# Decoder of two layers on one core: the first mixture's routing moved into the MLP, its rows merged back by VectorE

## Chip, core, metric
One core of one Trainium2 chip. The metric is the device time of one execution in microseconds, from the program's start to its end. Lower is better. The program is one hand-written instruction stream per engine (TensorE, VectorE, ScalarE, GpSimd, SyncE), with semaphores between them.

## What is computed
x is [4, 512, 256] (2048 tokens of 256), the context [4, 1601, 256], all fp32. Two layers, each of a Mamba mixer, a cross attention and a feed-forward, with residuals and norms between them. The change is around the first layer's feed-forward, a mixture of eight experts with one expert for each token and room for 512 tokens in each:

```python
x_flat = (x_normed @ W_proj + b_proj).reshape(N, d)
routing_weights = softmax(x_flat @ W_gate)
ew, ei = top_k(routing_weights, 1); ew = ew / ew.sum()        # weight of the one choice
masked = where(ei == e, ew, -1); top_scores, top_idx = top_k(masked, 512)   # per expert
h = gelu(layernorm(x_flat[top_idx] @ W1 + b1)); out_e = h @ W2 + b2
outputs = zeros.at[top_idx].add(out_e * w)
x = x + layernorm(outputs) * ln_g + ln_b
```

Ahead of it stands the first layer's cross attention with its own MLP (256 to 1024 to 256 with a gelu), behind it the second layer's Mamba mixer: projection, convolution with 4 taps, silu, x projection, dt (softplus), a scan over 512 tokens for 512 channels x 16 states, gate, output projection.

## The kernel before
**Order.** `build` (L3415) strings seven stages, with a barrier between two: mixer A (0 to 555 us), keys of the first attention (to 970), queries and MLP (to 1278), experts of the first mixture (to 1609), mixer B (to 2145), second attention (to 2540), second mixture. `barrier` (L3409) drains each engine and waits for all five, so what is issued behind a barrier, a DMA too, starts only then. SBUF tiles and semaphores of a stage are given on to the next.

**MLP and gate** (`queries_pe`, `queries_dve`, `queries_act`, L1212 to L1501). Per batch of 512 tokens TensorE makes 8 hidden products, then 4 output tiles; woven in are the gate's steps of the batch before: transposes of the normalized rows (`gate_turned_pe`, at hidden product 4), projection to XF, transposes of XF, logits. VectorE begins a batch with the statistics of X (`x_stats_dve`), the affine rows of the next batch (`rows2`), the reciprocal, and the gate's normalized rows fn. Behind the loop stands the last batch's gate, with nothing beside it.

**Routing** (`experts_dve` L2039 to L2073, `ranks_pe`). After the barrier, for all 16 tiles of 128 tokens at once: first maximum, one-hot marks, softmax weight (Exp on ScalarE), ranks by two products with a triangle and with ones, running totals by 15 dependent adds, slot number, two lists of indices. GpSimd scatters 16 tiles of XF into m0buf by indirect DMA (L1805), SP waits for all (L1787) and loads expert 0's rows. Before this SP has issued both weights of expert 0.

**Expert loop** (`experts_pe`, `experts_act`, `experts_dve`). Every product is three fp32r products of high and low halves (`mm3`, L107). Per expert: W1 and W2 are cast to high halves by ScalarE and the low halves made by VectorE; 4 hidden tiles of [128, 1024] are drawn by VectorE with b1 (L2017) and their statistics taken (L2022); `hidden_norm` normalizes them (L2037); 8 times transposes, gelu and cast on ScalarE (L1945, L1950), low half on VectorE (L2098); 4 output tiles, drawn with b2 to ob (L2114), stored by ScalarE's queue to m0res in slot order. The hidden products of the next expert are woven between the transposes of this one.

**Merge** (L1808 to L1814, L2117 to L2150). GpSimd waits for all stores, then gathers 16 tiles of XF from m0res by indirect DMA. ScalarE multiplies by the weight, VectorE takes statistics, normalizes with ln_g, adds to X, and takes the statistics of the new X for mixer B.

**Mixer B's start** (`mamba_sp`, `mamba_dve`, `mamba_act`, `mamba_pe`). After the barrier SP loads the four weights; TensorE waits for the last of them (L393). Normalized rows xn, transposes, input projection of four blocks, four convolutions on VectorE (`mamba_conv_dve`, 4 operations each), silu, x projection, dt, softplus, first decays, then the scan of 128 units with VectorE at 3.46 us each. B and C rows go to DRAM and come back broadcast over partitions, by SP.

## Time and profile before

| what | us |
|---|---|
| median of 3 runs (lowest, highest) | 2915.48 (2909.48, 2918.29) |
| the profiled execution's own time | 2914.07 |
| its span, first to last instruction | 2912.2 |
| TensorE busy | 2417.0 (83%) |
| VectorE busy | 2194.8 (75%) |
| ScalarE busy | 1444.4 (50%) |
| GpSimd busy | 894.5 (31%) |
| granted TensorE clock, mean | 0.910 of full |
| chain that ended last | PE 49%, DVE 28%, ACT 10%, issue 8%, POOL 2%, DMA 1% |

The sum of a forecast is made against 2914.07. PE is TensorE, DVE VectorE, ACT ScalarE, POOL GpSimd, SP SyncE; a name with q is the engine's queue. "L1805" is a line of the kernel before. out<-in are tile names without their numbers. A busy share says little where stages have different bounds: the chain and the windows by stage say more.

### The profile page before, as it was taken

The numbers are of one execution on the slowest core, as the hardware profiler recorded it, in microseconds if no ns is written. First come the engines' busy times: TensorE is split into PE (matmuls) and PEld (weight loads), VectorE is DVE, ScalarE is ACT, GpSimd is POOL, SyncE is SP. The second block draws the span as 40 slices with busy tenths as digits, with TensorE's granted clock in tenths as the row PEclk, the third lists the DMA queues.
The fourth block names the chain that finished last, engine by engine and source line by source line (L and its number), as shares of the span: only waits on it lengthen the run. The fifth ranks groups of instructions, "written<-read, shape, count | busy, mean of one in ns | idle before, by whom it ended". The sixth has DMA issues, their size and how long they took to land.

```text
span 2912.2 us, 31513 instructions
## 1 busy us (share of the span) xinstructions
PE 2417.0 (83%) x10888; PEld 1575.3 (54%) x10888; DVE 2194.8 (75%) x3180; ACT 1444.4 (50%) x2547; POOL 894.5 (31%) x617
## 2 busy tenths in 40 slices
PE   4989886588998899947993698988668888899998
PEld 1333332266776565736993233343234443799998
DVE  4999999688997365336995599999956653567776
ACT  5666564254665222213673565656412445356663
POOL 2868776300000000020002377877611235100004
PEclk7999999899999799978997699999987887889999
DMA  4031130380000000023331303203054231246652
GB/s 171 1 116 55 62 117 0 118 288 23 23 1 1 35 1 1 0 89 112 110 129 44 139 4 112 98 19 117 0 81 94 51 100 59 86 149 218 218 207 91
DMA packets 99065, 243.12 MB, mean 83 GB/s; under 512 B 9182, under 2 KB 63339, under 8 KB 91740
## 3 DMA queue, kind: packets, MB, share of 16 engines
q1 hardware_dynamic: 82540, 216.20, 22.7%
q10 hardware_dynamic: 11760, 12.32, 1.6%
q0 software_dynamic: 4608, 12.59, 1.4%
q8 instruction: 87, 1.43, 0.2%
q14 instruction: 70, 0.57, 0.1%
HBM read 187.93 MB, written 46.66 MB: 81 GB/s over the span
## 4 chain that ended last, share of the span: by engine, by line
PE 49%; DVE 28%; ACT 10%; issue 8%; POOL 2%; DMA 1%; ACTq 0%; DVEq 0%; SPq 0%; POOLq 0%
DVE psum L635 11%; PE psum L109 6%; PE psum L111 6%; PE psum L432 6%; PE psum L110 6%; PE psum L116 3%; DVE ch L643 3%; PE psum L397 3%; ACT WH L3119 2%; PE psum L1265 2%; PE psum L1279 2%; ACT g L3266 2%; PE psum L1249 2%; PE psum L2575 1%; PE psum L1227 1%
## 5 line engine op out<-in xcount | busy, mean ns | idle before, releaser
L317 POOL TENSOR_TENSOR bu<-u,row 128x1024 f32<-128x1024 f32 x254 | 597.0, 2355 | 289.0 <-DVE psum L635 190.9
L432 PE MATMUL psum<-ch,ident 128*128 128x512 f32 x1024 | 510.1, 627 | 137.9 <-DVE ch L643 137.3
L635 DVE TENSOR_TENSOR_SCAN psum<-psum,bu 128x1024 f32<-128x1024 f32 x256 | 585.5, 2287 | 18.8 <-ACT psum L514 18.6
L432 PEld LDWEIGHTS psum<-ch,ident 128*128 128x128 f32 x1024 | 188.5, 196 | 426.7 <-DVE ch L643 245.0
L514 ACT ACTIVATE psum<-dt,A 128x511 f32<-128x511 f32 x512 | 332.4, 682 | 0.4
L643 DVE TENSOR_TENSOR ch<-psum,row 128x1024 f32<-128x1024 f32 x256 | 313.0, 1223 | 7.6
L1535 POOL IOTA i<- 128x128 f32 x1 | 0.3, 345 | 710.2 <-DVEq L3411 710.2
L397 PE MATMUL psum<-hT,inw 128*128 128x512 f32 x256 | 140.7, 682 | 42.8 <-ACT sz L474 27.3
L3266 ACT ACTIVATE g<-psum,bias 128x256 f32<-128x256 f32 x248 | 101.2, 470 | 133.7 <-PE psum L111 126.0
L109 PE MATMUL psum<-WH,hs 128*128 128x256 f32 x496 | 145.3, 293 | 4.7 <-DVE hs L3346 2.3
L109 PE MATMUL psum<-xT,WH 128*128 128x256 f32 x496 | 142.3, 287 | 7.6 <-DVE xT L3309 7.6
L111 PE MATMUL psum<-xT,WH 128*128 128x256 f32 x496 | 141.7, 286 | 0.0
L110 PE MATMUL psum<-xT,WH 128*128 128x256 f32 x496 | 141.6, 286 | 0.0
L3346 DVE TENSOR_TENSOR hs<-g,hs 128x512 fp32r<-128x512 f32 x124 | 85.6, 693 | 73.5 <-ACT hs L3273 71.4
L111 PE MATMUL psum<-WH,hs 128*128 128x256 f32 x496 | 140.8, 284 | 0.0
L110 PE MATMUL psum<-WH,hs 128*128 128x256 f32 x496 | 140.3, 283 | 0.0
L3088 POOL DMA_INDIRECT R<-m1res,gi x26 | 26.2, 1007 | 340.0 <-DMA m1res<-ob 323.8
L511 ACT COPY psum<-zero 128x2 f32<-128x2 f32 x256 | 41.2, 161 | 175.3 <-DVE ch L643 174.4
L2650 ACT ACTIVATE pT<-psum 128x1024 f32<-128x1024 f32 (+3 forms) x128 | 87.5, 706 | 76.6 <-PE psum L2560 76.0
L2863 POOL TENSOR_SCALAR_AFFINE_SELECT pT<-pT 128x256 f32<-128x256 f32 x128 | 53.5, 422 | 230.6 <-ACT pT L2650 229.5
L3127 DVE TENSOR_TENSOR WH<-W,WH 128x1024 fp32r<-128x1024 f32 x96 | 113.1, 1220 | 7.8 <-ACT WH L3119 7.8
L397 PEld LDWEIGHTS psum<-hT,inw 128*128 128x128 f32 x256 | 54.2, 217 | 116.5 <-issue 63.7
(403 smaller groups left out, 5907.6 us busy)
## 6 DMA issues: line engine op xcount, KB each, us to landing
W<-in_m1W SPq DMA_DIRECT2D x24, 2052.0 KB, 8.6
row<-Ascr SPq DMA_DIRECT2D x64, 512.0 KB, 4.8
row<-Bscr SPq DMA_DIRECT2D x64, 512.0 KB, 4.8
m1buf<-zt SPq DMA_DIRECT2D x8, 2048.0 KB, 16.7
W<-in_m0W SPq DMA_DIRECT2D x16, 1024.0 KB, 5.0
xe<-m1buf SPq DMA_DIRECT2D x23, 256.0 KB, 8.2
m1res<-ob ACTq DMA_DIRECT2D x23, 256.0 KB, 5.0
m0buf<-zt SPq DMA_DIRECT2D x16, 256.0 KB
```

What stands on the lines that cost most here:

```text
L109: pe.matmul(o, al, bh, start=start, stop=False)
L110: pe.matmul(o, ah, bl, start=False, stop=False)
L111: return pe.matmul(o, ah, bh, start=False, stop=stop)
L317: e.tensor_tensor(m.bu[i % 3][:, :, :], u, m.row[:, g, 0, :, :], ALU.mult).then_inc(*m.fed.up)
L397: p = pe.matmul(bank, m.inw[:, f, 128 * ob:128 * ob + 128], m.hT[:, f, :], start=f == 0, stop=f == 1)
L432: p = pe.matmul(m.y, k.ident, m.ch[i % RING_C][:, j, :], start=False, stop=g == UNITS - 1 and j == 1)
L514: e = act.activation(a[:, j, 1:T], m.dt[:, s % SIX, 1:T], ACT.Exp, scale=m.A[:, n:n + 1])
L635: dve.tensor_tensor_scan(flat, flat, m.bu[i % 3][:, :, :].rearrange("p a n -> p (a n)"), 0.0, ALU.mult, ALU.add).then_inc(*m.scan.up)
L643: dve.tensor_tensor(m.ch[i % RING_C][:, :, :], a, m.row[:, g, 1, :, :], ALU.mult).then_inc(*m.out.up)
L2650: act.activation(m.pT[n % 6][:, :, 0:W], m.st[n % 2][:, :, 0:W], ACT.Exp, scale=0.25).then_inc(*m.ex.up)
L3127: dve.tensor_tensor(lo, w, hi, ALU.subtract).then_inc(*m.Wl.up)
L3266: e = act.activation(g[:, 256 * o:256 * o + 256], m.hb[j][:, 256 * o:256 * o + 256], ACT.Gelu_apprx_tanh, bias=m.bias[w % 3][:, 2 * j + o: ...
```

## The change
1. **Choice per batch in the MLP.** `gate_marks_dve`, `gate_exp_act`, `gate_ranks_pe`, `gate_slots_dve` do the routing of batch b-1 inside the MLP's iteration b (marks after logits, slots after the last output tile, ranks behind TensorE's last output tile) and of the last batch behind the loop, ahead of the barrier. GpSimd scatters batches 0 to 2 in the MLP (`mlp_pool`), batch 3 after the barrier.
2. **XF and m0buf rows get two columns**, the token's weight and its home number, and travel with the row.
3. **Expert 0's W1 and W2** are loaded in the MLP, when the last attended tile is out.
4. **The final norm moves to the experts' rows.** The weighted row's norm is taken on ob (statistics on VectorE, scale w/dev with the variance taken as w*w*var, applied by ScalarE; for the last expert by VectorE), and GpSimd scatters each expert's four tiles straight to their tokens' rows in m0res, which was cleared to zero. Half of the hidden normalization goes from VectorE to ScalarE. X + ln_b is added during expert 7.
5. **Mixer B** loads m0res as four blocks, VectorE multiplies with ln_g and adds to X; batch 0 first, batches 1 to 3 after the convolutions. Its weights are loaded during expert 2.
6. **Both mixers** make the fourth convolution on TensorE.
7. **First loads before the barrier**: wk, the first three context tiles and two ln rows for the keys, wk and the first context of the second attention.

```diff
@@ queries_dve, end of an MLP iteration
         out(4 * b + 2, bank["t2"])
         if b:
             gate_logits_dve(k, g, dve, b - 1, bank["lg"])
+            gate_marks_dve(k, g, dve, b - 1)
         out(4 * b + 3, bank["t3"])
+        if b:
+            gate_slots_dve(k, g, dve, b - 1, bank["rk"])
...
+def mlp_pool(k, m, g, pool):
+    gate_consts_pool(k, g, pool)
+    for b in range(B - 1):
+        gate_scatter_pool(k, g, pool, b)
...
+def gate_marks_dve(k, m, dve, b):
...
+    first_of_four_dve(k, m, dve, m.lg[:, s, :], m.m1[:, s], m.oh[:, s, :])
+    dve.tensor_scalar(m.end[:, :], m.ix[:, :], float(CAP), float(CAP * (E + 1)), ALU.mult, ALU.add).then_inc(*m.marks.up)
+    dve.tensor_tensor(m.sm[:, :, :], m.lg[:, s, :], wide4(m.m1[:, s]), ALU.subtract).then_inc(*m.sm_in.up)
...
+def gate_slots_dve(k, m, dve, b, bank):
+    dve.wait_ge(*m.sm_exp(b))
...
+    dve.wait_ge(*m.counted(b))
+    for t in range(4):
+        n = 4 * b + t
+        dve.tensor_tensor(m.tot[:, n + 1, :], m.tot[:, n, :], bank[:, 32 + E * t:32 + E * t + E], ALU.add).then_inc(*v.up)
+        done()
...
+    dve.tensor_tensor(m.XF[:, s, D], m.ws[:, :], m.keep[:, s], ALU.mult)
+    dve.tensor_copy(m.put_i[:, s], m.slot[:, s]).then_inc(*m.put.up)
@@ experts_pool
+    def tags(e):
+        pool.wait_ge(*m.xe_in(e))
...
+        pool.tensor_tensor(m.tf[:, e, :], m.room[:, e, :], m.xe[:, :, D + 1], ALU.add).then_inc(*m.tf_in.up)
+        pool.tensor_copy(m.tw[:, e, :], m.xe[:, :, D])
+        pool.tensor_tensor(m.t2[:, e, :], m.xe[:, :, D], m.xe[:, :, D], ALU.mult)
+        pool.tensor_scalar(m.tn[:, e, :], m.xe[:, :, D], -1.0, None, ALU.mult)
+        pool.wait_ge(*m.tf_in(e))
+        pool.tensor_copy(m.ti[:, e, :], m.tf[:, e, :]).then_inc(*m.tagged.up)
...
+    for e in range(E):
+        if e + 2 < E:
+            tags(e + 2)
+        if e:
+            out_scale(e - 1)
+            pool.wait_ge(*m.o_n(e - 1))
+            for t in range(4):
+                out_home(e - 1, t)
+        if e + 1 < E:
+            out_var(e)
+    for t in range(4):
+        pool.wait_ge(*m.o_last(t))
+        out_home(E - 1, t)
@@ hidden_norm on ScalarE and VectorE
+        for t in (2, 3):
+            h = m.hN[e % 2][:, t, :]
+            a = act.activation(h, h, ACT.Identity, scale=m.hrs[e % 2][:, t:t + 1], bias=m.hnb[e % 2][:, t:t + 1])
...
+        for t in range(2):
+            normed(dve, hN[:, t, :], hN[:, t, :], mv, m.hrs[e % 2], t).then_inc(*m.h_n.up)
@@ experts_sp
+        if e == 2:
+            mamba_weights_sp(k, following, sp)
+    for home in m.home:
+        sp.wait_ge(*home(2 * E - 1))
@@ mixer B
+def mamba_home_dve(k, m, dve, b):
+    x, rows = k.X[:, 4 * b:4 * b + 4, :], mamba_home(m, b)
+    dve.wait_ge(*m.home_in[b](0))
+    dve.tensor_tensor(rows, rows, k.zt[:, 0:1, :].to_broadcast([128, 4, D]), ALU.mult).then_inc(*m.times.up)
+    dve.wait_ge(*m.times(b))
+    dve.tensor_tensor(x, x, rows, ALU.add).then_inc(*m.home.up)
+    dve.wait_ge(*m.home(b))
+    x_stats_dve(k, dve, 4 * m.rnd + b)
...
-    for ob in range(4):
+    for ob in range(3):
         mamba_conv_dve(k, m, dve, ob)
+    if m.rnd:
+        for j in range(1, B):
+            mamba_home_dve(k, m, dve, j)
@@ mamba_act, unit loop
+        if m.rnd and i == 1:
+            for j in range(1, B):
+                x_stats_act(k, act, 4 * m.rnd + j)
```

`mamba_home` is the region of the B/C rows, in which the four blocks of m0res land before those rows are loaded; SP waits for the last addition before it goes on.

## Rows read from the trace of the kernel before
**Rows 1.** Windows of MLP, expert loop, second hole: stretch, length, PE PEld DVE ACT POOL busy, PEclk, DMA.
```profile
1125.00:1268.00 143.00, 137.87 (x562) 97.04 (x562) 54.69 (x144) 39.56 (x55) 0.00 (x0) 0.98 0.00 1
...
1340.00:1561.00 221.00, 210.50 (x1407) 192.20 (x1405) 183.01 (x290) 139.19 (x189) 0.00 (x0) 0.97 0.32 111
1561.00:1602.00 41.00, 0.00 (x0) 0.00 (x0) 29.10 (x97) 9.77 (x23) 16.71 (x16) 0.52 0.22 64
```

**Rows 2.** The chain of waits, routing. Columns: start us, us, what.
```profile
1278.13 0.19 DVE lg L1751
...
1281.09 1.28 ACT L1929
...
1284.12 0.17 DVE tot L1574
...
1310.27 2.40 DMA m0buf<-XF,puti
1312.68 3.70 DMA xe<-m0buf
```

**Rows 3.** The chain of waits, merge and second mixer's start.
```profile
1559.79 1.43 DVE ob L2114 x4
...
1616.26 3.80 PE psum L397 x4
```

**Rows 4.** Timeline of GpSimd, its third scatter. Columns: start us, us, engine, line, operation, idle.
```profile
1292.84 1.95 POOL L1805 DMA_INDIRECT m0buf<-XF,puti  x1 [0.30 <-issue]
```

**Rows 5.** The chain of waits, first loads of both attentions.
```profile
555.87 4.90 DMA gT<-in_x0wk
...
2145.10 3.86 DMA cT<-in_x1ctxT
```

**Rows 6.** Timeline of VectorE beside GpSimd: keys' start, routing.
```profile
565.51 2.15 DVE L904 SCALAR_TENSOR_TENSOR XF<-XF,cmv,bc 128x256 f32<-128x256 f32 x1
...
1289.28 2.41 DVE L1992 TENSOR_TENSOR W1s<-W,W1s 128x1024 fp32r<-128x1024 f32 x2
```

**Rows 7.** Timeline of VectorE in the MLP, third and fourth batch.
```profile
1197.88 1.38 DVE L150 TENSOR_SCALAR fn<-X,xmv,xrs 128x256 f32<-128x256 f32 x4
...
1233.08 0.18 DVE L140 RECIPROCAL xrs<-xsd 128x4 f32<-128x4 f32 x1 [3.62 <-ACT xsd L146]
```

**Rows 8.** Timeline of TensorE in the MLP and behind its end.
```profile
1200.29 1.04 PE L116 MATMUL psum<-ident,fn 128*128 128x128 f32 x8
...
1241.73 3.62 PE L1683 MATMUL psum<-wp,fT 128*128 128x256 f32 x16
...
1265.13 1.55 PE L116 MATMUL psum<-ident,fn 128*128 128x128 f32 x8 [3.31 <-DVE fn L150]
1267.52 6.34 PE L1683 MATMUL psum<-wp,fT 128*128 128x256 f32 x16 [0.83 <-ACT fT L1707]
```

**Rows 9.** Timeline of VectorE across one expert boundary.
```profile
1423.17 2.98 DVE L150 TENSOR_SCALAR hN<-hN,hmv,hrs 128x1024 f32<-128x1024 f32 x4
...
1435.32 0.69 DVE L2098 TENSOR_TENSOR hs<-g,hs 128x512 fp32r<-128x512 f32 x1 [0.57 <-ACT hs L1950]
```

**Rows 10.** Timeline of all engines at the program's start.
```profile
0.82 2.10 SPq L3475 DMA_DIRECT2D X<-in_x  x4
...
4.97 1.41 DVE L129 BATCH_NORM_STATS2 xst<-X 128x6 f32<-128x256 f32 x4 [4.97 <-DMA X<-in_x]
```

**Rows 11.** Groups by line in the expert loop, ScalarE's cast of 128x1024.
```profile
L1908 ACT CAST W1s<-W 128x1024 fp32r<-128x1024 f32 x12 | 11.9, 1039 | 0.0
```

**Rows 12.** Timeline of VectorE, second mixer's start.
```profile
1609.70 1.39 DVE L150 TENSOR_SCALAR xn<-X,xmv,xrs 128x256 f32<-128x256 f32 x4 [0.33 <-DVEq L3411]
...
1629.74 2.33 DVE L330 SCALAR_TENSOR_TENSOR xc<-xs,PV,xc 128x512 f32<-128x512 f32 x3
1646.13 0.69 DVE L297 TENSOR_TENSOR dt<-dt,xs 128x512 f32<-128x512 f32 x1 [14.06 <-ACT xs L482]
...
1652.39 2.30 DVE L635 TENSOR_TENSOR_SCAN psum<-psum,bu 128x1024 f32<-128x1024 f32 x1 [3.19 <-ACT psum L514]
```

More of the change, by code:

```diff
@@ L205, in mamba_make @@
     n = PER * B
-    m.w = c(L + "weights", 4, 16)
+    m.w = k.next_w if rnd else c(L + "weights", 4, 16)
+    if rnd:
+        m.home_in, m.home = [c(L + f"rows_home{b}", 1, 16) for b in range(B)], c(L + "x_plus_rows", B)
+        m.times = c(L + "rows_times", B)
     m.zeros = c(L + "zeroed", 2)
@@ L281, in mamba_sp, with mamba_home @@
     sp.dma_start(m.outw[:, :, :], d[L + "outw"]).then_inc(*m.w.up)
+def mamba_home(m, b):
+    return m.row[:, b, 0, :, :].rearrange("p a (t c) -> p (a t) c", c=D)
+def mamba_sp(k, m, sp):
+    if m.rnd:
+        for b in range(B):
+            sp.dma_start(mamba_home(m, b), k.DR["m0res"][T * b:T * b + T, :].rearrange("(t p) c -> p t c", p=128)).then_inc(*m.home_in[b].up)
+        sp.wait_ge(*m.home(B - 1))
+    else:
+        mamba_weights_sp(k, m, sp)
     for b in range(B):
@@ L637, in mamba_dve @@
             mamba_gate_dve(k, m, dve, s - 1)
+        if m.rnd and i == 4:
+            for j in range(1, B):
+                x_inverse_dve(k, dve, 4 * m.rnd + j)
         if n == 5 and b + 1 < B:
+            if m.rnd:
+                dve.wait_ge(*k.inv_dev(4 * m.rnd + b + 1))
             mamba_rows_dve(k, m, dve, b + 1)
@@ L1630, in ffn0_make @@
[L1630 to L1634 removed]
+    m.xb = c("m0x_plus", B)
     return m
@@ new lines, in gate_exp_act, with gate_ranks_pe @@
+def gate_exp_act(k, m, act, b):
+    act.wait_ge(*m.sm_in(b))
+    act.activation(m.sm[:, :, :], m.sm[:, :, :], ACT.Exp).then_inc(*m.sm_exp.up)
+def gate_ranks_pe(k, m, pe, own, b):
+    bank = own.bank(pe)
+    if b == 0:
+        pe.wait_ge(*m.consts(0))
+    pe.wait_ge(*m.marks(b))
+    rows = m.oh[:, 4 * b:4 * b + 4, :].rearrange("p t e -> p (t e)")
+    pe.matmul(bank[:, 0:32], m.tri[:, :], rows, start=True, stop=True)
+    pe.matmul(bank[:, 32:64], m.ones[:, :], rows, start=True, stop=True).then_inc(*m.counted.up)
+    own.freed_by(m.ranked(b))
@@ L1847, in last_out_pe @@
     if o == 0:
-        pe.wait_ge(*m.W2l(2 * e + 1))
+        for j in range(2):
+            pe.wait_ge(*m.W2l[j](e))
     pe.wait_ge(*m.hl(8 * e + o))
@@ L1888, in experts_pe @@
             columns_pe(k, m, pe, own, e + 2)
-        pe.wait_ge(*m.W2l(2 * e + 1))
+        for j in range(2):
+            pe.wait_ge(*m.W2l[j](e))
         for t in range(4):
@@ L1926, in hidden_norm, with out_dev, out_rows @@
         act.activation(m.hsd[e % 2][:, :], m.hmv[e % 2][:, :, 1], ACT.Sqrt, bias=k.eps).then_inc(*m.h_sd.up)
-    act.wait_ge(*m.sm_in(0))
-    act.activation(m.sm[:, :, :], m.sm[:, :, :], ACT.Exp).then_inc(*m.sm_exp.up)
-    own.use()
-    own.use()
+        act.wait_ge(*m.h_nb(e))
+        for t in (2, 3):
+            h = m.hN[e % 2][:, t, :]
+            a = act.activation(h, h, ACT.Identity, scale=m.hrs[e % 2][:, t:t + 1], bias=m.hnb[e % 2][:, t:t + 1])
+        a.then_inc(*m.h_na.up)
+    def out_dev(e):
+        act.wait_ge(*m.o_var(e))
+        act.activation(m.osd[:, :], m.osd[:, :], ACT.Sqrt, bias=k.eps).then_inc(*m.o_sd.up)
+    def out_rows(e):
+        act.wait_ge(*m.o_sc(e))
+        for t in range(4):
+            o = m.ob[e % 2][:, t, :]
+            a = act.activation(o, o, ACT.Identity, scale=m.osc[:, t:t + 1], bias=m.onb[:, t:t + 1])
+        a.then_inc(*m.o_n.up)
     first_split(0)
@@ L2056, in experts_dve @@
-    dve.wait_ge(*v.last())
-    dve.tensor_scalar(m.keep[:, :], m.rank[:, :], float(CAP), None, ALU.is_lt)
-    dve.tensor_scalar(m.slot[:, :], m.ix[:, :], float(CAP), None, ALU.mult).then_inc(*v.up)
-    dve.wait_ge(*v.last())
-    dve.tensor_tensor(m.slot[:, :], m.slot[:, :], m.rank[:, :], ALU.add).then_inc(*v.up)
-    dve.wait_ge(*v.last())
-    dve.wait_ge(*m.own_in(0))
-    dve.tensor_tensor(m.slot[:, :], m.slot[:, :], m.own[:, :], ALU.subtract).then_inc(*v.up)
-    dve.wait_ge(*v.last())
@@ L2100, in experts_dve @@
                 step(rows)
+            if e + 1 == E and o % 2:
+                b = o // 2
+                if b == 0:
+                    dve.wait_ge(*m.vecs(1))
+                x = k.X[:, 4 * b:4 * b + 4, :]
+                dve.tensor_tensor(x, x, m.ln_b[:, :].unsqueeze(1).to_broadcast([128, 4, D]), ALU.add).then_inc(*m.xb.up)
         if e + 2 < E:
@@ L3433, in build @@
         k.xsd, k.xrs = k.make([128, NT], name="xsd"), k.make([128, NT], name="xrs")
-        for n, rows, got in (("m0", TRASH + N, TRASH + 1), ("m1", ROOM * E + 256, 256 * NTILE)):
-            dram(n + "buf", [rows, D])
-            dram(n + "res", [got, D])
+        dram("m0buf", [TRASH + N, D + 2])
+        dram("m0res", [N + TRASH, D])
+        dram("m1buf", [ROOM * E + 256, D])
+        dram("m1res", [256 * NTILE, D])
         c = k.count
```

482 lines of the change are left out of this document (250 added, 232 removed).

## Prediction
> **What bounds the kernel now.** I read the page's chain first, then the windows cut at the stage borders [rows 1], then the chain in order of time across the two holes that the page's slices show in TensorE's row. In the first, 1278 to 1316, the chain runs over GpSimd and DMA [rows 2]; in the second, 1561 to 1602, TensorE is busy for 0 of 41 us. The MLP (137.9 of 143.0) and the expert loop (210.5 of 221.0) are TensorE's; the two scans, not shown, are VectorE's and nothing in the change touches their steady state. So the change is judged by what it takes out of the two holes and what it adds to the two full stretches.
>
> First hole: from the last logits (1278.33) to the first expert's transposes (1316.43) are 38.1 us: choice and ranks 10.7, sixteen scatters from 1289.3 on, the landing 2.40, the load of the rows 3.70 [rows 2]. Second hole: the last expert's output at 1559.79 to the second mixer's input projection at 1616.26, 56.5 us [rows 3]: store, sixteen gathers, weighting, a norm for 16 tiles, and a weight load that is issued only after the barrier.
>
> **The change part by part** (against the profiled execution's 2914.07 us, span 2912.2; the median of the runs is 2915.48, so 1.4 us above it; 0.3% is 8.7 us).
>
> *Choice per batch.* What stays on the path is the last batch. Small VectorE operations take 0.17 us and follow each other at 0.2 [rows 2]. After the last logits: seven operations to marks and differences 1.4; Exp 0.4 (its table load now stands behind a copy of ScalarE that ended earlier, so it goes ahead of the wait; before it was on the path with 1.28 [rows 2]); four for the weight 0.85; four sums 0.8; ten to the indices 2.0; sum 5.45, plus 0.4 for the barrier, now behind the choice, and GpSimd's start. Four scatters instead of sixteen: of the old sixteen the first three were slow (1.23, 1.70 and 1.95 [rows 4], with 0.3 between), so the last one starts 5.8 after the first; if they ran at the later pace (0.96+0.30) it would be 3.8. Landing 2.4, rows 3.7, transposes 0.1. The W1 load of expert 1 and its bias row now come just ahead of the rows in SP's queue instead of 20 us earlier; I take 1.5 for that, between 0 and 5 (the 1 MB load of wk took 4.90 [rows 5]). New 19.35, gain **18.8** (15 to 22). Expert 0's splits (two of W1, two of W2, 1.2 us each on VectorE [rows 6]) start at the barrier and end 6 us later, hidden by scatter, landing and rows (13.4 us); without that cover they would cost 5. The early W1 and W2 loads run in the MLP, where DMA is idle (share 0.00 [rows 1]).
>
> *What it costs the MLP.* Per batch VectorE gets marks (1.4) between two output tiles, which is hidden: TensorE needs 3.5 us for an output tile, and VectorE waits for it. The slot part (0.85+0.8+2.0 = 3.65) stands after the last output tile, ahead of the next batch's statistics. With the batch that has the affine rows behind it, the last normalized rows end at 1199.2 and TensorE takes them at 1200.29 [rows 7, 8]; they come at 1202.85 and TensorE at 1200.7, less the 0.6 of transposes that already run: a stall of 1.5. In the last batch the square root waited for ScalarE's gelus (3.62 idle on VectorE [rows 7]): no stall. After the last batch slots(2) stand in front of the statistics, all on the path: 3.65. Two rank products in TensorE's queue: 0.8. Together **-6.0** (-3 to -13). GpSimd's three batches of scatters are hidden: it has nothing to do in the MLP [rows 1], and a batch's scatters take 7 us of its 35.
>
> *Expert loop.* VectorE is nearly full: per 26.9 us expert it stands idle 1.7 us, in four pieces, the longest 0.57 before an hs [rows 9]. It loses two of four normalizations (2.98/2 = 1.5 [rows 9]), and gets four statistics of the output and their aggregates (1.7: four of 1.41 together [rows 10] and 0.3), a reciprocal and a shift (0.4). ScalarE takes the two tiles (1.04 each, as its cast of 128x1024 [rows 11]) ahead of W1's high half, so VectorE waits about 1.2 for that, which its other work used to fill. Following one boundary: W1's low half ends 0.7 late, the statistics put W2's low half 1.9 late, the next two hs 0.9 late, and from there on VectorE has no gap until the output products need the last hs. Cost 0.9 per expert, six boundaries 5.4, and 1.0 in the last expert (its chain W2, gelu, hs is exposed: TensorE has no next expert's products to fill in). **-6.4** (0 to -14). The four additions of ln_b (1.2 each) go into the last expert's idle VectorE (1.2 to 4.0 between its hs). ob's buffers: a scatter ends a full expert before its buffer is used again.
>
> *Merge.* After the last ob: expert 6's scatters first. Its square root needs a table (1.28+0.3 after the last cast), scale on GpSimd 1.2, rows on ScalarE 1.7: 1563.0. Four scatters 6.5, expert 7's four 5.0, landing 2.4: 1577.0 (expert 7's own statistics and normalization end at 1566, hidden by the queue). Barrier and first of four loads: the first statistics of the program began at 4.97 with the load issued at 0.82 [rows 10], so 4.15: 1581.2. Multiply and add 2.5, statistics 1.7, square root and reciprocal 0.6: xn at 1586.1 against 1609.70 [rows 12], **23.6**. From xn to the x projection, which waited for the fourth convolution's silu, were 23.1 us, 3.8 of them the wait for the weights, now issued during expert 2. TensorE makes the fourth convolution; ScalarE must still build the diagonals (4.9) before it draws, then three convolutions of 2.83 (0.5 and 2.33 [rows 12]) and two silus: x projection at xn+19.4 instead of xn+23.1, **+3.7**; TensorE is then less cold: **+1.0** (0 to 2.7). Rows of batches 1 to 3: 4.2 each, 12.6 on VectorE, covered by the 14 us in which it waited for softplus [rows 12], and the B/C spill now waits for them on SP: the first input then comes 0.1 before its decay, so nothing is lost, with 0 to 3 as bound. Three square roots at unit 1 cost two table loads and 0.9, 3.5 on ScalarE, of which TensorE's z products hide half; with the reciprocals **-2.4** (0 to -4). Sum **+25.9** (19 to 31).
>
> What the row shows of a table load is 1.28 us, and the activation came 0.02 us behind it [rows 2]. The Trainium skill (ScalarE: Activation LUTs, What ACT_TABLE_LOAD costs) gives about 2.66 us for every switch, the drain included. By that the two added switches at unit 1 would cost 2.8 more and the sum be 2.8 smaller. I stay with the row.
>
> *The rest.* First mixer: one convolution less on VectorE 2.83, one silu more behind it 0.6: **+2.2**. Keys: wk's load of 4.90 [rows 5] goes in front of the barrier: **+5.0**; GpSimd's 4.5 us split stays, and VectorE's row beside it (2.15 for 0.48 [rows 6]) moves with it. Second attention: 3.86 and the issue, **+4.1** [rows 5]. The wider clear of m0res (2 MB) goes beside the keys' arithmetic, where what is queued behind it, the third batch's context, is not needed before the second batch's keys are done (the four batches take 390 us): nothing; uncovered it would cost its own 2 MB, about 2 loads of 4.90.
>
> Sum: 18.8-6.0-6.4+25.9+2.2+5.0+4.1 = **43.6**; 2914.1-43.6 = 2870.5, **2871**.
>
> **The rivals.**
> 1. *The full stretches give way less* (0.17): ScalarE's share of the normalization frees the loop, and the slots fall into slack. For it: VectorE loses 1.5 us where its queue is longest. Against: no gap left in the o loop. Without both costs but slots(2): 43.6+6.4+2.0 = 52, **2862**.
> 2. *They give way more* (0.22): TensorE stalls in two MLP batches and its clock falls to the lower level behind each, as behind the 3.31 us wait, where sixteen projection records took 6.34 instead of 3.62 [rows 8]; that is 3 more behind each of the two and 3 for the second stall itself, and the loop costs 2.0 per expert instead of 0.9, because ScalarE's two tiles come later than I take them. 43.6-9-7 = 28, **2886**. Against: the granted clock of the MLP is 0.98 with short waits in it [rows 1].
> 3. *The program gets slower* (0.03): GpSimd's tags and scatters hold VectorE in the loop. A VectorE operation beside GpSimd's tensor operation took 2.15 instead of 0.48 [rows 6]. Four indirect DMAs (1.26 to 2.2) and some eight small operations are 7 to 10 us per expert. If VectorE stood for all of it, eight times 8 is 64: 2914.1-50+64 = **2928**; it decides from 6.3 us per expert. Against: beside the slow scatters at 1289 two VectorE splits took 2.41, 1.2 each as elsewhere [rows 6]; GpSimd was the one slowed.
> 4. *The scatters are not early at all* (0.03): if batch 2's scatters queued past the barrier, four more would be on the path, +5: **2876**, inside the forecast's own range.
>
> **How the numbers follow.** The forecast has 0.55: 2863 to 2880 by the bounds of its terms. The range reaches into rivals 1 and 2: **2856 to 2890**. Faster by over 0.3% is everything but rival 3 and the far end of rival 2: 0.95; within it 0.02; slower 0.03.
>
> **What would show it.** Last logits to first transposes near 19 us, with four m0buf scatters behind the barrier and twelve before. MLP stretch 6 us longer, TensorE waiting 1 to 2 us for fn in the third batch. Expert period 27.8 instead of 26.9, TensorE waiting for hs. From the last ob to the first input projection 30 instead of 56.5; xn waiting for the home load; eight scatters in a row. From the last ob to the second mixer's first scan 64 us instead of 92.6 [rows 3, 12], VectorE idle under 2 us before softplus. Wrong if the loop grows by over 2 us per expert, or if the home loads take over 8 us after the last scatter.

## Result and profile after

The kernel after takes **2863.36 us** (median of 4 runs, 2860.25 to 2868.16), the kernel before 2916.75 in the same measurement: ratio 0.9825, 95% interval 0.9805 to 0.9844. The profiled execution of the kernel after took 2868.16, the slowest of the four, span 2866.4; the one of before 2914.07, span 2912.2. So the two executions that can be compared row by row differ by 45.9 us (45.8 in span), the medians by 53.4. The forecast's sum was 43.6, and its 2871 is 7.6 above the median after, which lies at the lower edge of the forecast's own band (2863 to 2880) and nearer to rival 1's 2862; the traced execution lies nearer to the forecast. The range 2856 to 2890 holds both.

The page of the kernel after: span, busy time by engine, the chain's shares by engine.

```profile
span 2866.4 us, 31778 instructions
...
PE 2427.0 (85%) x10916; PEld 1577.8 (55%) x10916; DVE 2190.2 (76%) x3228; ACT 1483.2 (52%) x2592; POOL 928.6 (32%) x703
...
PE 47%; DVE 30%; ACT 12%; issue 9%; DMA 1%; POOL 1%; ACTq 1%; POOLq 0%; DVEq 0%; SPq 0%
```

TensorE is busy as long as before (2417.0 then), in 45.8 us less: what went is idle time of TensorE. The chain moved from TensorE (49 to 47%) to VectorE (28 to 30%). The rest must be read hole by hole. First the chain across the routing (start us, us, what), which answers to [rows 2]:

```profile
1275.28 0.24 ACT sm L1733
1278.88 0.72 issue
1279.60 0.96 POOL m0buf L1716
...
1282.39 1.97 POOL m0buf L1716
...
1284.66 5.86 DMA m0buf<-XF,puti
1290.54 3.66 DMA xe<-m0buf
1294.34 1.95 PE psum L116 x8
```

Exp takes 0.24 with no table ahead of it. Four scatters stand behind the barrier and twelve in the MLP. The last of them starts 5.06 behind the first, nearer to the forecast by the slow pace of [rows 4] (5.8) than to the one by the fast pace (3.8), but its landing takes 5.86 where [rows 2] had 2.40.

The chain across the merge and the second mixer's start, which answers to [rows 3]:

```profile
1543.89 2.08 ACT ob L2109 x4
...
1546.24 0.99 POOL m0res L1966
...
1547.53 0.96 POOL m0res L1966
...
1548.63 10.47 POOLq L3557
1559.12 3.92 DMA row<-m0res
...
1567.92 0.42 DVE xn L150
...
1595.62 1.71 DMA Bscr<-xd
...
1597.73 6.49 DMA row<-Bscr
...
1605.64 2.31 DVE psum L688
```

Behind ScalarE's scaling of expert 6 stand eight scatters in GpSimd's queue (the piece of 10.47 us covers six of them and their landing), then the barrier and the load of one block. The last three lines are new: the first scan is now released by the rows of B and C from DRAM, which SP could spill only behind VectorE's last addition.

How the difference of 45.8 us lies along the program (us, each stretch between the same two operations in both traces, gain positive):

| stretch | before | after | gain | forecast |
|---|---|---|---|---|
| first mixer, start to first scan | 59.22 | 56.67 | 2.55 | 2.2 |
| its 128 scans | 480.30 | 478.71 | 1.59 | 0 |
| output product to first key product | 24.11 | 19.13 | 4.98 | 5.0 |
| keys, attention, MLP to last logits | 708.13 | 712.77 | -4.64 | -6.0 |
| last logits to first transposes | 38.30 | 20.70 | 17.60 | 18.8 |
| experts, to last ob | 243.36 | 248.85 | -5.49 | -6.4 |
| last ob to xn | 49.91 | 24.73 | 25.18 | 23.6 |
| xn to x projection | 23.08 | 18.51 | 4.57 | 3.7 |
| x projection to first scan | 19.61 | 19.21 | 0.40 | 1.0 |
| second mixer from first scan to output | 482.36 | 487.66 | -5.30 | -2.4 |
| from there to second attention | 14.30 | 10.00 | 4.30 | 4.1 |
| rest | | | 0.06 | 0 |

Every term that was forecast has its sign. The one furthest off is the second mixer's steady part. The stretches miss their terms by 11.6 us if all misses are counted as positive and by 2.2 in sum, so the close sum is in part luck. The 7.5 us by which the medians differ more than the two executions are in no trace that can be laid beside another; how far executions of one code stand apart is seen below.

### The profile page after: what moved, and what is told of

The parts are those of the page before. It is cut to its first block, busy times and chain, and to the rows that moved or that the text cites. A ratio compares the mean times of both kernels' runs of the same rounds, so it can differ in the third digit from the quotient of the medians.

```text
span 2866.4 us, 31778 instructions
## 1 busy us (share of the span) xinstructions
PE 2427.0 (85%) x10916; PEld 1577.8 (55%) x10916; DVE 2190.2 (76%) x3228; ACT 1483.2 (52%) x2592; POOL 928.6 (32%) x703
## 4 chain that ended last, share of the span: by engine, by line
PE 47%; DVE 30%; ACT 12%; issue 9%; DMA 1%; POOL 1%; ACTq 1%; POOLq 0%; DVEq 0%; SPq 0%
DVE psum L688 11%; PE psum L462 7%; PE psum L109 5%; PE psum L111 5%; PE psum L110 5%; PE psum L116 3%; DVE ch L701 3%; PE psum L425 3%; ACT g L3412 2%; ACT WH L3265 2%; PE psum L1346 2%; PE psum L1332 2%; PE psum L1316 2%; PE psum L2717 2%; PE psum L1294 2%
## 5 line engine op out<-in xcount | busy, mean ns | idle before, releaser
L2845 DVE TENSOR_REDUCE mp<-psum 128x1 f32<-128x128 f32 (+1 forms) x192 | 85.6, 506 | 40.5 <-PE psum L2619 40.4
```

## Experiments

Whole times do not resolve 3 us here: in four kernels below (W1's high half first, normalization all on VectorE, W1 behind the rows, slots later), which are identical behind the second mixer's last scan, the stretch from there to the end took 770.9, 783.1, 775.8 and 785.6 us on one chip. In the kernel after it took 779.5 us and in its second execution 788.6. So each single edit is read in the stretch from the last output tile of the MLP's second batch (1183.12 in the kernel after; one expectation below calls it the third's) to the second mixer's first scan (1605.64). It holds everything that the edits touch, bar the mixers' scans and the first mixer's start. It is 460.5 us in the kernel before and 422.5 in the kernel after. Three executions in which its code is the same took 422.5, 422.1 and 421.7, so differences under 0.8 us say nothing.

| kernel | that stretch | against after | program |
|---|---|---|---|
| after, run once more | 422.1 | -0.4 | 2879.57, ratio 0.9821 |
| W1's high half first | 416.8 | -5.7 | 2861.45, ratio 0.983 |
| normalization all on VectorE | 416.8 | -5.7 | 2861.57 (one run) |
| W1 behind the rows | 418.8 | -3.7 | 2863.15 (one run) |
| slots later | 419.0 | -3.5 | 2872.33 (one run) |
| additions first | 420.2 | -2.4 | 2876.98 (one run) |
| root early | 419.6 | -2.9 | 2868.7 (one run) |
| scatters late | 434.1 | +11.6 | 2899.54 (one run) |
| fourth convolution on VectorE | 425.2 | +2.6 | 2869.7 (one run) |
| filler in the scans | 421.7 | -0.8 | 2875.01 (one run) |
| four edits | 410.1 | -12.4 | 2863.6, ratio 0.9792 |
| five edits | 409.0 | -13.5 | 2861.83, ratio 0.9769 |

The last column comes from four chips and can't be compared across them. Beside the four kernels named above the kernel before took 2917.85 us, beside additions first, root early, scatters late and four edits 2925.09, beside fourth convolution and filler 2917.57, beside five edits and the kernel after run once more 2929.93.

### The loop: what costs 0.9 per expert
The forecast had the period, from one expert's last output tile to the next one's, at 27.8, and it is 27.77. Its cause as forecast: ScalarE's two tiles put W1's low half 0.7 late, the output statistics make the rest. VectorE and ScalarE at one boundary of the kernel after:

```profile
1374.16 1.53 DVE L150 TENSOR_SCALAR hN<-hN,hmv,hrs 128x1024 f32<-128x1024 f32 x2
1377.70 2.36 DVE L2157 TENSOR_TENSOR W1s<-W,W1s 128x1024 fp32r<-128x1024 f32 x2 [2.00 <-ACT W1s L2076]
```
```profile
1374.28 2.38 ACT L2098 ACTIVATE hN<-hN,hnb,hrs 128x1024 f32<-128x1024 f32 x2 [0.44 <-DVE hnb L2201]
1376.57 1.98 ACT L2076 CAST W1s<-W 128x1024 fp32r<-128x1024 f32 x2
```

VectorE is done with its half at 1375.7 and stands 2.00 us until ScalarE has cast W1's first half behind its own two tiles. Two kernels take that wait away in different ways.

```diff
@@ experts_act
         if e + 1 < E:
             hidden_norm(e + 1)
         if e + 2 < E:
             first_split(e + 2)
+        if e + 1 < E:
+            hidden_rows(e + 1)
...
@@ experts_pe
-        pe.wait_ge(*m.h_n(2 * e + 1))
-        pe.wait_ge(*m.h_na(e))
         for o in range(8):
...
+            if o == 0:
+                pe.wait_ge(*m.h_n(2 * e + 1))
+                pe.wait_ge(*m.h_na(e))
```
`hidden_rows` is the two tiles, taken out of `hidden_norm`, which keeps the root.

> Edit: in the expert loop ScalarE casts W1's high half ahead of its two hidden tiles, and TensorE waits for the normalized rows only behind the first hidden product of the next expert. In the kernel after, VectorE stands 2.00 us idle per expert until that cast (1375.7 to 1377.7) and TensorE starts the next W1 product 0.4 us behind W1's low half. Theory (the loop's loss is this one wait): W1's low half starts 1.8 us earlier, the period falls from 27.77 to 26.4 (26.0 to 26.8; below that TensorE is full), last ob 8 us earlier, program 2855. Rival (VectorE's queue is full elsewhere, the wait only moves to the output rows): period 27.5 to 27.8, program 2861 to 2863.

```diff
@@ hidden_norm
-        for t in (2, 3):
-            a = act.activation(h, h, ACT.Identity, scale=..., bias=...)
...
-        for t in range(2):
+        for t in range(4):
             normed(dve, hN[:, t, :], hN[:, t, :], mv, m.hrs[e % 2], t)
```


> Edit: the hidden normalization goes back to VectorE whole, as before the change; everything else stays. Theory (half of it on ScalarE buys nothing, since VectorE then waits 2.00 us for W1's high half behind ScalarE's two tiles): VectorE's normalization ends at 1377.3 instead of 1375.7, the cast is ready by then, W1's low half starts within 0.4 us of where it started, and the period is 27.4 (27.2 to 27.8) against 27.77. Rival (VectorE's busy time sets the period, so its 1.6 us count in full): period 29.2 to 29.4, last ob 9 to 10 us later.

Measured: the period is **26.95** with the cast first and **26.97** with the whole normalization on VectorE; before the change it was 26.91. From the first copy of the rows to the last ob it is 241.7 in both against 246.9, the last expert's 1.2 included. Both forecasts missed: the first had 26.0 to 26.8 and the last ob 8 us earlier, the second 27.2 to 27.8. In the first kernel W1's low half starts 2.07 us behind the root instead of 4.16, in the second 3.52, and the period is the same, since TensorE is then full: busy 26.97 of the 26.97 us of a period in the second kernel, 27.20 of 27.77 in the kernel after. VectorE of the second kernel:

```profile
1371.33 2.98 DVE L150 TENSOR_SCALAR hN<-hN,hmv,hrs 128x1024 f32<-128x1024 f32 x4
1374.22 2.36 DVE L2151 TENSOR_TENSOR W1s<-W,W1s 128x1024 fp32r<-128x1024 f32 x2
...
1377.82 1.40 DVE L2204 BATCH_NORM_STATS2 ost<-ob 128x6 f32<-128x256 f32 x4
```

VectorE has no idle time ahead of W1's low half, and the statistics of the output (1.40) are in the period as well. So the output norm costs the loop next to nothing (26.97 against 26.91), and the 0.8 per expert, 5.2 in sum, comes from the half that was handed to ScalarE, by its place ahead of the cast: the first kernel leaves that half on ScalarE, behind the cast, and loses nothing either. What was meant as relief is the cost. "VectorE's busy time sets the period" (29.2) fell clearly: 1.45 us more of normalization on VectorE (2.98 for 1.53) made each expert 0.8 shorter.

### The landing of 5.86 us
```diff
@@ experts_sp
-    first_in(1)
     sp.wait_ge(*k.gate.sent(NT - 1))
     rows_in(0)
+    first_in(1)
     rows_in(1)
```


> Edit: SP issues expert 1's W1 and bias row behind expert 0's rows instead of ahead of the wait for the scatters. Theory (the scatters' landing took 5.86 us instead of 2.40 because the 1 MB of W1 was in flight beside it): landing 2.4 to 3, rows 3.7, last logits to first transposes 17.0 instead of 20.5, expert 1's W1 still lands before its cast at 1313, program 3.5 us shorter. Rival (the landing is long for another reason, the last scatters' own writes or the other row loads): landing 5 to 6, nothing gained.

The chain of that kernel (start us, us, what):

```profile
1286.89 2.53 DMA m0buf<-XF,puti
1289.43 3.68 DMA xe<-m0buf
1293.25 1.95 PE psum L116 x8
```

Landing 2.53, last index to first copy of the rows 14.35 instead of 17.67, and W1 was in time. The theory holds, with one addition: the line moves W1 (1 MB) and its bias row (0.5 MB), and the experiment does not part the two. The place of one line in SP's queue is worth 3.3 us.

The price of the early scatters alone:
```diff
@@ mlp_pool
-    for b in range(B - 1):
-        gate_scatter_pool(k, g, pool, b)
@@ experts_pool
-    gate_scatter_pool(k, k.gate, pool, B - 1)
+    for b in range(B):
+        gate_scatter_pool(k, k.gate, pool, b)
```


> Edit: GpSimd scatters all four batches behind the barrier, choice and slots stay in the MLP. It prices the early scatters alone. Theory (each scatter costs its place in GpSimd's queue; the landing of 5.86 us is W1's transfer): from the first of sixteen to the last 21 us as before the change instead of 5.1, landing 2.4 instead of 5.86 since W1 is long in, so last index to first copy of the rows 17.7 + 15.9 - 3.4 = 30.2. Rival 1 (the landing is long whatever is in flight): 33.6. Rival 2 (with the indices ready GpSimd goes faster than before the change, 1.26 each from the start): 28.

GpSimd's first, third and fifth scatter, and the load behind the last (chain):

```profile
1282.74 1.23 POOL L1714 DMA_INDIRECT m0buf<-XF,puti  x1 [313.99 <-DVEq L3556]
...
1286.00 1.96 POOL L1714 DMA_INDIRECT m0buf<-XF,puti  x1 [0.30 <-issue]
...
1289.52 0.96 POOL L1714 DMA_INDIRECT m0buf<-XF,puti  x1 [0.30 <-issue]
```
```profile
1306.01 3.58 DMA xe<-m0buf
```

The last scatter starts at 1303.45, 20.7 us behind the first, and its data is there 2.56 us later. Last index to first copy of the rows: **29.47**, forecast 30.2; in the kernel after 17.67. From the first scatter to the last it is 20.71 instead of 5.06; 3.3 of that went back with the landing, and 0.45 because the first scatter starts 0.5 instead of 0.96 behind the last index. That is 11.9, and 11.8 is measured, of the 17.6 that the routing gave. The rest is the choice, 10.7 to 5.0. The first three scatters are slow here too, as long as VectorE makes expert 0's splits (1283.62 to 1288.25); the fourth, at 1288.26, takes 0.96.

### The slots in the MLP
```diff
@@ queries_dve
+        if b >= 2:
+            gate_slots_dve(k, g, dve, b - 2, None, 1)
         if b:
             gate_projected_dve(k, g, dve, b - 1, bank["p0"], bank["p1"])
...
-            gate_slots_dve(k, g, dve, b - 1, bank["rk"])
+            gate_slots_dve(k, g, dve, b - 1, bank["rk"], 0)
```


> Edit: of the slot part in the MLP only the five additions that read TensorE's bank stay behind the last output tile; weight and slot number move behind the next batch's affine rows and sums (batches 0 and 1) and behind the last batch's first transposes (batch 2), where VectorE waits 3.6 to 4.6 us for TensorE's projection. Theory (the slots stand on the path in the third batch and behind the last): third batch 36.79 to 35.7, from the last output tile to the last logits 18.95 to 16.9, together 3.1 us (2.5 to 3.5) shorter. Rival (the third batch is late by its rank products and by TensorE's clock, not by the slots; the tail moves alone): third batch 36.5 or more, together 2.1.

TensorE of the kernel after at the third batch's normalized rows and behind the loop:

```profile
1192.54 1.37 PE L116 MATMUL psum<-ident,fn 128*128 128x128 f32 x8 [0.43 <-DVE fn L150]
...
1261.11 1.96 PE L116 MATMUL psum<-ident,fn 128*128 128x128 f32 x8 [5.89 <-DVE fn L150]
```

TensorE waits 0.43 in the third batch and 5.89 behind the loop (3.31 before, [rows 8]). With the edit the third batch takes 35.86 instead of 36.79 and the last output tile to the last logits 16.32 instead of 18.74. But the last batch's index comes 5.59 behind the logits instead of 5.00, for a wait that the weight's four operations used to fill:

```profile
1274.31 0.75 DVE L1765 TENSOR_TENSOR tot<-tot,psum 128x8 f32<-128x8 f32 x4 [1.12 <-PE psum L1747]
```

Together 2.8 by these three, inside 2.5 to 3.5. The stretch of the table is 3.5 shorter; the other 0.7 lies in the experts, which the edit does not touch.

### The merge: root early
```diff
@@ experts_act: expert 6's root behind W2's high half, its rows behind expert 7's second gelu
+        if e == E - 2:
+            out_dev(e)
@@ experts_pool
             out_scale(e - 1)
+            if e == E - 2:
+                out_var(e)
             pool.wait_ge(*m.o_n(e - 1))
```


> Edit: expert 6's square root goes ahead of the last gelu table, its scale and its rows (ScalarE) between expert 7's second and third gelu, GpSimd takes its variance ahead of expert 5's scatters; so expert 6's four scatters leave during expert 7 instead of behind the last output. Theory (the eight scatters in a row are the merge's path): the first of the last four starts 4.5 us behind the last ob instead of 8.2, from last ob to xn 21.0 instead of 24.7; the last expert gets 0.5 longer (0.3 to 1.5), net 3.2. Rival (the square root pushes the last gelus back, whose chain is exposed): last expert 2 or more longer, net under 1.5.

ScalarE at the last gelu table, and GpSimd's fourth scatter of expert 6 and first of expert 7:

```profile
1521.46 0.30 ACT L2105 ACTIVATE osd<-osd,t 128x4 f32<-128x4 f32 x1 [1.17 <-POOL osd L1954]
1521.77 1.28 ACT L2127 ACT_TABLE_LOAD   x1
```
```profile
1534.76 0.96 POOL L1966 DMA_INDIRECT m0res<-ob,ti  x1 [0.30 <-issue]
1548.62 0.96 POOL L1966 DMA_INDIRECT m0res<-ob,ti  x1 [12.90 <-DVE ob L150]
```

From last ob to xn 21.29 instead of 24.73; the last expert is 1.2 longer, since ScalarE stands 1.17 us for GpSimd's variance and the gelus behind it are exposed. Net 2.2 up to xn. The four input projections behind xn ran 1.1 us longer in this execution (TensorE's granted clock 0.50 from 4 to 8 us behind xn, 0.65 in the kernel after). That is not the edit's doing for certain: they ran 1.0 longer in the two kernels of the loop too, which do not touch them. It did not reach the first scan either, which waits for the rows of B and C: from last ob to first scan 58.58 instead of 62.45. Neither the theory (3.2) nor the rival (under 1.5) is exact; the queue of eight was the path, and a third of what it gives goes back.

### The second mixer's start
```diff
@@ mamba_home_dve
-    dve.wait_ge(*m.home(b))
-    x_stats_dve(k, dve, 4 * m.rnd + b)
@@ mamba_dve
...
         for j in range(1, B):
             mamba_home_dve(k, m, dve, j)
+        for j in range(1, B):
+            dve.wait_ge(*m.home(j))
+            x_stats_dve(k, dve, 4 * m.rnd + j)
```


> Edit: in the second mixer's start the three multiply-and-add pairs of batches 1 to 3 run one behind the other and their statistics behind all three (they stood between the additions). In the kernel after, SP spills the B and C rows only behind the last addition (ends 1595.6) and VectorE waits 5.68 us for them; the decay of unit 0 was ready at 1603.4, the scan began at 1605.64. Theory (the moved rows put the spill on the path): last addition 3.4 us earlier, rows 3.4 earlier, then the first decay is the later one, scan 2.1 us earlier: from the x projection's copy to the first scan 13.4 instead of 15.5. Rival (the spill's landing does not follow the addition, or the decay is later than it looks): 15 to 15.5. The stretch of 128 scans, 481.3 us, stays within 1 us in both.

VectorE at the first scan of the kernel after, and with the additions first:

```profile
1604.32 1.22 DVE L345 TENSOR_TENSOR bu<-u,row 128x1024 f32<-128x1024 f32 x1 [5.68 <-DMA row<-Bscr]
1605.64 2.30 DVE L688 TENSOR_TENSOR_SCAN psum<-psum,bu 128x1024 f32<-128x1024 f32 x1
```
```profile
1600.87 1.23 DVE L345 TENSOR_TENSOR bu<-u,row 128x1024 f32<-128x1024 f32 x1 [1.91 <-DMA row<-Bscr]
1603.77 2.30 DVE L691 TENSOR_TENSOR_SCAN psum<-psum,bu 128x1024 f32<-128x1024 f32 x1 [1.68 <-ACT psum L546]
...
1621.52 2.30 DVE L691 TENSOR_TENSOR_SCAN psum<-psum,bu 128x1024 f32<-128x1024 f32 x1 [2.47 <-ACT psum L546]
```

From the copy of the x projection to the first scan 13.39 instead of 15.55, as expected. The wait of 5.68 for the rows becomes 1.91 for the rows and 1.68 for the first decay. So the forecast's "nothing is lost" to the spill was wrong by 2.2. And a second wait appears that the forecast had priced: 2.47 us at unit 4, where ScalarE's roots and their two table loads (2.56) stand. In the kernel after it is hidden, since the decays had a head start while VectorE waited for DMA. The stretch of the table ends ahead of it, so it shows only the gain: the first seven scans take 31.37 us instead of 29.84, and of the 2.4 us that the edit gains up to the first scan 0.8 is left at the eighth.

```diff
@@ both mixers
-FIRST = [...] + [("conv", 3), ("xp", 0)] + [...]
+FIRST = [...] + [("xp", 0)] + [...]
@@ mamba_dve
-    for ob in range(3):
+    for ob in range(4):
         mamba_conv_dve(k, m, dve, ob)
```


> Edit: the fourth convolution goes back to VectorE in both mixers, everything else stays. Theory (the forecast's terms): in the second mixer VectorE convolves until 1587.9 instead of 1585.0, the x projection's copy comes 2.5 to 3 us later (from xn 25 instead of 22.2), and the additions behind it are 2.9 later and with them the spill, so the first scan is 2.9 later (from last ob 65.3 instead of 62.45); in the first mixer the first scan comes 2.2 later (58.9 instead of 56.7). Rival (the diagonals and the silu table on ScalarE set the x projection, not the convolution): under 1 us in both.

First mixer's first scan at 58.81 instead of 56.67: 2.14 for the forecast's 2.2. The direction is clear, the size is not: twelve executions with the same code up to there had it between 56.28 and 58.25, the two with the convolution on VectorE at 58.81 and 59.22. Second mixer: xn to the copy of the x projection 25.88 instead of 22.17, last ob to first scan 64.83 instead of 62.45, so 2.4 of the 3.7 reach the scan. The convolution set the x projection: it starts 20.67 behind xn instead of 18.51. The other 1.5 of the 3.7 is TensorE's clock: idle for 8.44 us through VectorE's fourth convolution, it is granted 0.69 over the x projection (1.00 in the kernel after), whose eight records take 5.17 instead of 3.62.

### 128 scans: 476 or 481 us
The forecast left the steady scans alone. They took 476.0 before and 481.3 after in the second mixer, 480.3 and 478.7 in the first. Unit by unit, the excess over 476.0 lies in the same five of the 128 (40, 48, 72, 80, 104), all but 1.2 us of it in the second mixer and all but 0.5 in the first. There TensorE is behind and VectorE waits for y.

```diff
@@ mamba_pe
+        if i > PER and i % PER == 7:
+            for _ in range(5):
+                pe.matmul(m.y, k.ident, m.zero[:, 0:1].to_broadcast([128, T]), start=False, stop=False)
         pe.wait_ge(*m.out(i))
```


> Edit: in both mixers, at unit 7 of the second, third and fourth batch, where TensorE stands idle 2.3 to 2.6 us because VectorE takes a batch's statistics, TensorE adds five products with zeros to y (0.43 us each, 2.15 in all) ahead of its wait. The result is unchanged. Theory (the five units 40, 48, 72, 80 and 104 are long because TensorE's granted clock falls to the lower level behind that idle stretch, 0.74 in 1760 to 1765 in the kernel after, and TensorE then is late with y): the 128 scans of the second mixer take 476 to 477.5 instead of 481.3, those of the first 475 to 476 instead of 478.7. Rival (TensorE is late by its work, and 2.15 us more make it later): 481 or more in both.

It gave 480.7 and 479.6, near the rival's 481, but not for its reason alone. TensorE's own row shows what the filler cost:

```profile
1761.73 4.47 PE L462 MATMUL psum<-zero,ident 128*128 128x512 f32 x10
```

A product of 128x512 is two records of 0.43; I had read one, so five take 4.47 us, not 2.15, and units 40 and 72 took 5.33 each, 1.4 more than the 3.91 that they take where nothing is late. The units behind (48 and 80) fell from 5.25 and 4.84 to 4.02. The cleaner evidence is the unchanged kernel run once more:

> The kernel after unchanged, on the same chip as the five edits. Ratio to the kernel before 0.9825 (0.980 to 0.985) as measured with the change; its stretch of 128 scans in the second mixer 481.3 within 0.5 us if its length comes from the program's own order, anywhere from 476 to 482 if it is the chip's.

Its second mixer took 478.2, its first 476.0. TensorE at the same unit in the two executions of the same code, the profiled one first; then the granted clock behind it (stretch, length, PE PEld DVE ACT POOL busy, PEclk, DMA share, GB/s):

```profile
1761.05 2.45 PE L462 MATMUL psum<-ch,ident 128*128 128x512 f32 x4 [2.61 <-DVE ch L701]
1763.29 3.16 PE L425 MATMUL psum<-hT,inw 128*128 128x512 f32 x4
```
```profile
1758.44 1.98 PE L462 MATMUL psum<-ch,ident 128*128 128x512 f32 x4 [2.61 <-DVE ch L701]
1760.27 1.88 PE L425 MATMUL psum<-hT,inw 128*128 128x512 f32 x4
```
```profile
1760.60:1765.60 5.00, 4.55 (x7) 2.02 (x8) 4.66 (x5) 2.32 (x5) 3.90 (x2) 0.68 0.00 0
```
```profile
1757.70:1762.70 5.00, 4.26 (x10) 2.01 (x11) 5.00 (x5) 3.13 (x8) 3.89 (x2) 1.00 0.00 0
```

The same idle stretch of 2.61 us, and in one execution the clock falls to the lower level behind it (0.68 over five microseconds) and the four records of the next projection take 3.16 instead of 1.88, in the other it stays at 1.00. Unit 48 then takes 5.25 against 4.01. So 3 us of the 5.3 that this stretch lost can come and go with the code unchanged. The two executions may have been on different chips, but the chip is not needed for it: on one chip four kernels with the same first mixer took 478.8, 476.1, 476.1 and 476.1 for its scans. How often the clock falls is another matter. Of seven executions in which the second mixer's start is that of the kernel after, with neither the additions nor the root moved, five took 481.3 to 481.6, and of the kernel before there is one trace (476.0), so that the change makes the fall more likely is neither shown nor excluded. Nor is the first mixer's 1.59 shown to be no gain: eleven executions with the fourth convolution on TensorE and no filler took 475.7 to 478.8, the two with it on VectorE 480.3 both times. What decides in which execution the clock falls is open.

### All together


> Edit: four of the single edits together: hidden normalization on VectorE alone, expert 1's W1 behind expert 0's rows, the slots' second part later, the additions first. By the stretches that they were seen or are expected to shorten: 5.2 + 3.3 + 2.7 + 2.1 = 13.3 us against the kernel after, 2850 (2844 to 2858; the stretch behind the second mixer varied by 15 us between kernels that do not differ there). Rival (they hide each other, since all shorten the time in which TensorE idles and its clock then falls deeper or less): under 8 us by the sum of their own stretches.

> Edit: the four edits of before and expert 6's early square root together. From the last output tile of the MLP's third batch to the first scan of the second mixer the kernel after takes 422.5 us (1183.1 to 1605.6), the one with four edits 410.1. Theory (the early root adds its 2.7 us to that): 407.5, and against the kernel after on the same chip 0.9945 (0.992 to 0.997). Rival (with a shorter loop the last expert's gelu chain takes the root's time whole): 410, 0.9955.

The four edits: the stretch 410.1, 12.4 shorter for the 13.3 expected; ratio to before 0.9792 (0.9768 to 0.9817). The edits nearly add up in this stretch. The median of 2863.6 is outside the expected 2844 to 2858, on a chip where the kernel before took 8.3 us more than beside the kernel after, and the first seven scans give back 1.5 here as well. The five: 409.0, ratio **0.9769** (0.9747 to 0.9790), beside 0.9821 (0.9797 to 0.9845) of the kernel after in the same measurement, that is 0.9947 of it. The early root adds 1.1 on top of the four, nearer to the rival: 1.3 to the last expert, 3.4 off the merge, and again 1.0 for the input projections at the lower clock. The version with five edits is faster than both kernels.

## Why the prediction was right, point by point

**What bounds.** Two holes of TensorE, filled from 38.3 to 20.7 and from 56.5 (last ob to input projection) to 28.3, against two full stretches. Right; the hole forecast at 30 is the merge's.

**Routing, 18.8 forecast, 17.6 measured.** The choice took 5.00 for 5.45, the four scatters 5.06 for 5.8. The queue extra, "I take 1.5 for that, between 0 and 5", was the term mis-sized: 3.3. GpSimd's start took 0.96 where the sum has 0.4 for it and the barrier. The cover for expert 0's splits held: they end at 1284.7, the rows are there at 1294.2.

**MLP, -6.0 and -4.64.** Slots(2) on the path took 3.06 (forecast 3.65), and the tail got 2.5 longer: the gate's projection ran in 5.47 instead of the 6.34 of [rows 8]. The forecast stall of 1.5 in the third batch was a wait of 0.43; with the clock and the rank products that batch is 1.38 longer, the fourth 0.45, the second 0.00. That the last batch has no stall was right.

**Loop, -6.4 and -5.49.** Period 27.77 for 27.8 and 1.3 for the last expert's 1.0: the size was right where it was paid. It was paid at five boundaries, not six: from expert 5's last output to expert 6's it is 26.67 us against 26.65 before. The mechanism was half right: the wait behind ScalarE is the whole cost, the output statistics are none of it, since TensorE sets the period of 26.9 once W1's low half is 0.6 earlier. Rival 1 said that the loop gives way less since ScalarE takes half the normalization; the opposite holds, that half is what it gives. Rival 2's 2.0 per expert did not come.

**GpSimd holding VectorE (rival 3).** Not in the loop: VectorE's operations there keep their lengths (hs 0.68 in both kernels, W1's low half 1.22). It does in two other places. One is the keys' start: the row of [rows 6] (0.48 alone, 2.15 before) takes 4.46 beside GpSimd's split of 4.50, at no cost, since the first key product comes 2.6 us behind the split's end in both kernels. The other is in the second mixer. The keys' row, then VectorE's four normalizations for batch 1, and GpSimd beside them:

```profile
554.08 4.46 DVE L963 SCALAR_TENSOR_TENSOR XF<-XF,cmv,bc 128x256 f32<-128x256 f32 x1
...
1625.43 5.55 DVE L150 TENSOR_SCALAR xn<-X,xmv,xrs 128x256 f32<-128x256 f32 x4
```
```profile
1625.73 4.77 POOL L345 TENSOR_TENSOR bu<-u,row 128x1024 f32<-128x1024 f32 x2
```

Alone the four take 1.39 [rows 12], before the change 3.39 beside one of GpSimd's products of 2.36, here 5.55 beside two (4.77): they stand until each product is done. That is 2.2 of the lost scans; a wait for a decay of 1.3, which stood there before, is gone. The Trainium skill (SBUF — State Buffer, SBUF: two separate sides) says that GpSimd and VectorE, the latter in operations of certain modes or with two inputs in SBUF, share a pair of ports that one of them holds for a whole instruction while the other blocks fully; the trace agrees, with 2.2 us for the second product. What GpSimd's scatters show below fits the same from the other side.

**Merge, +25.9 and 24.85.** Eight scatters in a row, 9.85 from the start of the first to the end of the last for my 11.5 in sum, and xn 25.2 earlier for 23.6. The x projection 4.57 for 3.7, of which the convolution is 2.2 by its own experiment; the other 2.4 went with the wait for the weights. That experiment's further 1.5 is the slower x projection itself, which the forecast had apart as 1.0. Two steps failed. "The B/C spill now waits for them on SP ... so nothing is lost, with 0 to 3 as bound" was 2.2, inside its bound. The -2.4 for roots and reciprocals was -5.3 in the trace, and of other causes: 4.1 in the five units where TensorE is late (most of it gone in the second execution), and 1.1 in the first seven scans, where the held normalizations cost 2.2 and a wait is gone. The roots' table loads cost nothing until the additions come first, and then 2.5.

What the trace has for a table load is again 1.28, and in the kernel with the additions first the two loads and the roots between them take 3.3 us of ScalarE, of which 2.47 reached VectorE. The Trainium skill (ScalarE: Activation LUTs, What ACT_TABLE_LOAD costs) gives about 2.66 for each switch with its drain; an estimate from that is 5.3 for the two. The trace does not agree: the activation starts 0.01 to 0.02 us behind the load, and the load 0.01 to 0.03 behind the operation ahead of it.

**The small terms.** Keys 4.98 for 5.0, second attention 4.30 for 4.1, first mixer 2.55 for 2.2: read from one row each, and within 0.4. For the first mixer that closeness is luck, since its start varies by 2 us between executions of the same code.

**Open.** The medians differ by 53.4 and the sum of traced stretches by 45.8. The stretch behind the second mixer alone varied by 15 us between four kernels that are the same there, and by 9 between two executions of the kernel after, so this can be the choice of executions; it was not shown.

## What to carry to other kernels
Handing half of a busy engine's work to another engine pays only if nothing that the first one needs stands behind it in the other's queue: here two tiles on ScalarE, ahead of a cast that VectorE waits for, cost 0.8 us per expert. The last transfer issued ahead of a wait is the one to look at: 1.5 MB that nobody needed for 30 us doubled the landing of the scatters that everybody waited for. And judge an edit of 3 us by the stretch that it touches, in the same operations of two traces: whole times carry 15 us from stretches that it does not touch. But look past the end of that stretch too: moving the additions gained 2.4 us up to the first scan and gave 1.5 back in the seven behind it.

## What was not expected of the hardware
- The granted clock behind the same 2.61 us of idle TensorE is 0.68 in one execution and 1.00 in another, of the same code. Over the first mixer's 128 scans thirteen executions of the same scan code took 475.7 to 480.3 us, and 478.8 at most with the fourth convolution on TensorE.
- Four indirect scatters land 2.53 us behind the last one's start, and 5.86 us beside loads of 1.5 MB that SP issued between them; their own times on GpSimd stay (0.96, 1.23, 1.97 and 0.96, 1.23, 1.96).
- An indirect scatter takes 0.96 us on GpSimd and, but for one that began 0.4 us ahead of them, 1.2 to 2.0 beside VectorE's splits of expert 0, in a burst of 4 as in one of 16, and 0.96 from the first scatter after the splits' end (1288.26 in the kernel with the late scatters).
